# A four-layer transformer stack on one core: loops written out, weights loaded earlier, and steps moved in three stages

## The chip, the cores and the metric

The kernel runs on one core of a Trainium2 chip. The metric is the device time of one execution in microseconds (us). The engines are TensorE (PE), VectorE (DVE), ScalarE (ACT), GpSimd (POOL) and SyncE (SP, which here issues DMAs only).

## The reference, cut to what is computed

The input `x` is 8 items of 256 tokens of 256 features. Four layers each add an attention-like part and a feed-forward part and normalise after each:

```python
x = _layernorm(x + _L0_attn_ref(x, ...))   # RMS norm, Mamba-2 chunked scan (4 heads), gated
x = _layernorm(x + _L0_ffn_ref(x, ...))    # int8 weights: silu(x@Wg*s) * (x@Wu*s) @ Wd*s, 256 -> 1024 -> 256
x = _layernorm(x + _L1_attn_ref(x, ...))   # 16 heads of 128, softmax(q k^T / sqrt(128)) v @ w_o
x = _layernorm(x + _L1_ffn_ref(x, ...))    # mixture of experts
x = _layernorm(x + _L2_attn_ref(x, ...))   # Mamba scan, 512 channels x 16 states
x = _layernorm(x + _L2_ffn_ref(x, ...))    # ternary weights, silu(gate)*up, RMS norm, projection
x = _layernorm(x + _L3_attn_ref(x, ...))   # causal attention with one k and v for 16 heads, then a GELU MLP
x = _layernorm(x + _L3_ffn_ref(x, ...))    # gated, with low-rank experts
```

The mixture of experts in layer 1:

```python
_, sel = jax.lax.top_k(sigmoid(x2d @ gate_w.T), 4)            # 4 of 32 experts for each token
w = softmax(x2d @ gate_w.T)[sel]; w = w / w.sum(-1)
def _moe(x2d, Wg, Wu, Wd, cw):                                # Wg, Wu: (experts, 256, inner)
    a = silu(einsum('th,ehi->eti', x2d, Wg)) * einsum('th,ehi->eti', x2d, Wu) * cw.T[:, :, None]
    return einsum('eti,eih->th', a, Wd)
large = _moe(x, Wg, Wu, Wd, cw_large)                         # 32 experts, inner 96
small = _moe(x, cWg, cWu, cWd, cw_small)                      # 16 chunks (expert // 2), inner 128
return large + 0.05 * small
```

## The kernel before

`X` stays in SBUF. The program is a list of eight phases, `l0_attn` to `l3_ffn` (l0a, l0f, l1a, l1f, l2a, l2f, l3a, l3f in the names), and each ends at a barrier of all engines. A phase has its own buffers, and one function for each engine. The order on an engine is the order of the code, and semaphores join the engines. In all phases but l1f and l2a an engine's function is `item(0)`, `item(1)` in straight code and then `with engine.Fori(...)` over pairs of items, a loop on the engine whose body is two items (`p` picks one of two buffers).

In the feed-forward phases an item goes in steps. POOL copies its rows of `X` to `xin` (`stage`), PE transposes them into PSUM `T` (`turn`), ACT rounds them to `xh` (`keep_high`), and DVE makes the rest `xl = T - xh` (`keep_low`), so that a product of full precision is two or three products in fp32r. PE then makes gate and up for block `f` of 128 inner features (`GU`), ACT the silu `gs`, DVE `a` (the product of both) and its low part `al`, ACT its high part `ah`; `down(i - 1)` makes the output `Y` of the item before from `ah` and `al` of all its blocks, between the blocks of this item. DVE adds the residual and takes the statistics (`residual`), POOL raises the variance to -1/2 (`rstd`), and DVE writes `X` (`normalize`, L165). DVE and ACT run in steps of one block, and the numbers in `if step == 4` set where such a piece stands. In l2f POOL also sums the squares of `a` block by block (`s`), for the RMS norm.

In l0f, the int8 weights are loaded to `raw` at the phase's start and DVE casts them (L887) to `wg`, `wu`, `wd`. `raw` then serves as the ring for the weights `qkv` of l1a (`EarlyWeights`), which SP loads from there on.

In l1a an item is 16 heads, its products are L903, and the weights `wqkv` lie in two buffers `early_wqkv_h` and `early_wqkv` of 6144 columns (Q, K and V, 2048 each). The expert weights of l1f go to the same memory (`routes_over_low`, `routes_over_high`), so SP may load those for a range of columns only when the products that read these columns are over. `qk_ready` counts heads whose Q and K are made, `vc_ready` those with V. `wL[:, kc, expert, 0:192]` holds a large expert's gate (96) and up (96) side by side, `wS` the small chunks' (128 and 128), `dL` and `dS` the down weights. DVE's `routing` selects the experts of each item and numbers the tokens within each expert (`number`), and POOL scatters the rows of `X`, four copies per token, into the DRAM buffer `moe_x_rows` (`scatter`, four indirect DMAs for 128 tokens). This buffer is cleared by one DMA in l0a.

In l1f the last item's numbering and the scatters of items 6 and 7 are done first. DVE computes from the counts `n_e` a table of tiles (an expert and a place of rows for each of 95 tiles of 128 rows), SP stores it to DRAM (`moe_tiles`, L1393), reloads it as `rowi` and `rowp` (L1396), and then loads the rows of each tile (`xl`), which PE turns, multiplies with the weights of the tile's expert (L1475 large, L1478 small) and with the down weights (L1502, L1503).

In l3a step 9 of an item on ACT copies the transposed exponentials of a group of heads (`eT`, L2943) and then scales the next item's transposed input (`xT`, `keep_scaled`, L2895), which PE's projection (L2717) reads.

## Time and profile before

| what | us |
| --- | --- |
| median of three executions (lowest, highest) | 2623.26 (2620.5, 2629.05) |
| the profiled execution, its span | 2626.29, 2624.5 |
| PE busy | 2247.6, 86% of the span |
| DVE, ACT, POOL busy | 1699.0, 1443.6, 789.0 |
| bytes moved by DMA | 111.40 MB, 42 GB/s over the span |

The mean granted clock of PE is 0.932 of full speed. The phases lie, by the first instruction of each, at 0 (l0a), 258 (l0f), 400 (l1a), 939 (l1f), 1264 (l2a), 1855 (l2f), 2005 (l3a) and 2400 (l3f).

How to read it: busy times of the engines overlap, so none alone is the time. A row of the timeline gives start and duration, then engine, line, operation, `output<-inputs`, shape and a count of equal instructions run together; in brackets stands how long the engine was idle before it and what ended that. The table of waits sums these idle times by the pair of waiting line and releasing line.

### The profile page before, as it was taken

To read this page: it belongs to the slowest core of one execution; us is meant where nothing else is said; L and a number is where in the kernel's file an instruction comes from. 1 tells how busy PE (TensorE), PEld (TensorE's weight loads), DVE (VectorE), ACT (ScalarE), POOL (GpSimd) and SP (SyncE) were. 2 spreads that over 40 slices of the span, in tenths; PEclk is the share of its full clock that TensorE was granted. 3 is DMA by queue.
4 is the path that set the end of the run, shared out by engine and by line. 5 is a ranking of instruction groups with operands and counts; after the bars stand their busy time and mean duration, and the time that the engine had idled before them with its cause. 6 is when DMAs were issued, how large, how long until landed. Compare 5 with 4: busy or idle time off the path is not lost. (4 is left out here: it accounts for less than half of the span.)

```text
span 2624.5 us, 48418 instructions
## 1 busy us (share of the span) xinstructions
PE 2247.6 (86%) x15901; PEld 1944.7 (74%) x15909; DVE 1699.0 (65%) x4091; ACT 1443.6 (55%) x3765; POOL 789.0 (30%) x808
## 2 busy tenths in 40 slices
PE   6997878999999949999389889998686899987997
PEld 5875777999999939998166667767585566666886
DVE  4675776888787855552379888777465575663443
ACT  4664456777777713333377666775333565663332
POOL 1111000011111120000658777778484222221000
PEclk9888998999999969999689999999797999998999
DMA  4000111000000483332411111000300000000000
GB/s 131 1 0 13 45 54 33 1 18 18 18 18 18 103 223 114 119 103 86 130 41 49 50 47 43 33 34 1 115 0 1 1 1 0 0 0 1 1 0 32
DMA packets 98856, 111.40 MB, mean 42 GB/s; under 512 B 32330, under 2 KB 87235, under 8 KB 97621
## 3 DMA queue, kind: packets, MB, share of 16 engines
q1 hardware_dynamic: 91156, 87.23, 11.0%
q0 software_dynamic: 7488, 21.50, 2.6%
q8 instruction: 115, 1.88, 0.3%
q14 instruction: 97, 0.79, 0.1%
HBM read 79.73 MB, written 28.97 MB: 41 GB/s over the span
## 5 line engine op out<-in xcount | busy, mean ns | idle before, releaser
L1863 POOL TENSOR_TENSOR l2a_hb<-l2a_hb,l2a_Cb 128x1024 f32<-128x1024 f32 x128 | 303.1, 2379 | 112.9 <-DVE l2a_hb L2319 111.8
L2319 DVE TENSOR_TENSOR_SCAN l2a_hb<-l2a_dA,l2a_dB 128x1024 f32<-128x1024 f32 x128 | 288.3, 2274 | 62.6 <-PE l2a_dB L1944 26.8
L2173 ACT ACTIVATE l2a_dA<-l2a_delta,l2a_An 128x255 f32<-128x255 f32 x512 | 214.3, 497 | 37.3 <-DVE l2a_delta L2259 20.9
L1944 PE MATMUL l2a_dB<-l2a_diag,l2a_dxT 64*128 64x128 f32 x2048 | 188.8, 306 | 31.2 <-DVE l2a_hb L2319 18.4
L1944 PEld LDWEIGHTS l2a_dB<-l2a_diag,l2a_dxT 64*128 64x128 f32 x2048 | 139.8, 194 | 95.1 <-PE l2a_dB L1944 37.2
L903 PE MATMUL l1a_QK<-l1a_xh,early_wqkv_h 128*128 128x256 f32 x512 | 147.6, 288 | 11.1 <-issue 9.6
L903 PE MATMUL l1a_QK<-l1a_xh,early_wqkv 128*128 128x256 f32 x512 | 144.9, 283 | 0.0
L903 PE MATMUL l1a_QK<-l1a_xl,early_wqkv_h 128*128 128x256 f32 x512 | 144.8, 283 | 0.0
L1964 PE MATMUL l2a_YS<-ident,l2a_hb 128*128 128x128 f32 x1024 | 142.4, 286 | 1.0 <-POOL l2a_hb L1863 1.0
L1174 ACT ACTIVATE l1a_ex<-l1a_S,l1a_nm 128x256 f32<-128x256 f32 x256 | 119.3, 471 | 36.2 <-DVE l1a_nm L1226 36.2
L1964 PEld LDWEIGHTS l2a_YS<-ident,l2a_hb 128*128 128x128 f32 x1024 | 116.8, 146 | 12.2 <-POOL l2a_hb L1863 1.2
L2936 ACT ACTIVATE l3a_ex<-l3a_sm,l3a_nm 128x128 f32<-128x128 f32 (+1 forms) x256 | 99.0, 447 | 43.1 <-DVE l3a_nm L3073 42.4
L1209 DVE TENSOR_TENSOR l1a_qkl<-l1a_QK,l1a_qkh 128x512 fp32r<-128x512 f32 x128 | 88.3, 690 | 47.8 <-ACT l1a_qkh L1149 43.6
L1670 DVE TENSOR_TENSOR l1f_a<-l1f_s,l1f_GU 128x96 f32<-128x96 f32 x95 | 24.1, 254 | 138.8 <-ACT l1f_s L1540 138.8
L156 POOL TENSOR_TENSOR l1a_vpe<-l1a_mv,eps 128x2 f32<-128x2 f32 x8 | 1.5, 191 | 364.5 <-DVE l1a_mv L150 364.5
L903 PEld LDWEIGHTS l1a_QK<-l1a_xh,early_wqkv_h 128*128 128x128 f32 x512 | 98.1, 192 | 6.3 <-issue 6.3
L903 PEld LDWEIGHTS l1a_QK<-l1a_xl,early_wqkv_h 128*128 128x128 f32 x512 | 98.6, 193 | 5.2 <-issue 5.2
L3067 DVE TENSOR_TENSOR l3a_sm<-l3a_S,l3a_hide 128x512 f32<-128x512 f32 x96 | 65.7, 685 | 54.4 <-PE l3a_S L2786 54.3
L1478 PE MATMUL l1f_GU<-routes_over_high,l1f_xt 128*128 x380 | 98.3, 381 | 0.0
L903 PEld LDWEIGHTS l1a_QK<-l1a_xh,early_wqkv 128*128 128x128 f32 x512 | 98.2, 192 | 0.0
L1149 ACT CAST l1a_qkh<-l1a_QK 128x512 fp32r<-128x512 f32 x128 | 76.5, 598 | 35.0 <-PE l1a_QK L903 34.1
L2943 ACT COPY l3a_eT<-l3a_PT 128x512 f32<-128x512 f32 x96 | 55.4, 577 | 71.3 <-PE l3a_PT L2832 71.3
(657 smaller groups left out, 7427.3 us busy)
## 6 DMA issues: line engine op xcount, KB each, us to landing
l2a_Cb<-c_rows SPq DMA_DIRECT2D x8, 2048.0 KB, 7.0
l1f_xl<-moe_x_rows SPq DMA_DIRECT2D x95, 128.0 KB, 2.0
moe_y_rows<-l1f_yo SPq DMA_DIRECT2D x95, 128.0 KB, 1.7
l0f_raw<-in_L_attn_w_qkv_dram SPq DMA_DIRECT2D x24, 256.0 KB, 2.9
moe_x_rows<-X SPq DMA_DIRECT2D x1, 4224.0 KB, 17.3
l1f_dL<-in_L_ffn_Wd_dram SPq DMA_DIRECT2D x1, 3072.0 KB, 22.1
X<-in_L_attn_x_dram SPq DMA_DIRECT2D x8, 256.0 KB, 6.1
routes_raw<-in_L_attn_w_o_dram SPq DMA_DIRECT2D x4, 512.0 KB, 3.9
```

Of the source, the lines that this page charges most:

```text
L903: ins = pe.matmul(out, a, b, start=(first and n == 0), stop=(last and n == len(passes) - 1), **more)
L1149: nc.scalar.copy(qkh[:, h % 2].rearrange("p n t -> p (n t)"), QK[h % 2][:, :]).then_inc(qk_kept, 1)
L1174: last = nc.scalar.activation(ex[:, h % 2, j, :], S[h % 2][:, j * SEQ:(j + 1) * SEQ], ACT.Exp, bias=nm[:, h % 2, j:j + 1], scale=SCALE, ac ...
L1209: nc.vector.tensor_tensor(qkl[:, h % 2].rearrange("p n t -> p (n t)"), QK[h % 2][:, :], qkh[:, h % 2].rearrange("p n t -> p (n t)").bitcas ...
L1478: last = nc.tensor.matmul(GU[t % 2][:, 2 * EI:2 * (EI + SI)], xt[t % 2][:, kc, :], wS[:, kc, bass.ds(small, 1), :], start=(kc == 0), stop= ...
L1863: nc.gpsimd.tensor_tensor(h[:, :, :], h[:, :, :], Cb[p][:, s0:s0 + UN, :], ALU.mult).then_inc(hc_ready, 1)
L1944: last = nc.tensor.matmul(out[:, m:m + 2, j * P + a:j * P + a + HP], dxT[q][a:a + HP, j, c * P:(c + 1) * P], diag[q][a:a + HP, j, s0 + m:s ...
L1964: last = nc.tensor.matmul(YS[j][:, c * P:(c + 1) * P], hb[u % RING][:, n, j * P:(j + 1) * P], sh.ident[:, :], is_transpose=True, start=Fal ...
L2173: last = nc.scalar.activation(dA[(i * NU + u) % DAS][:, n, 1:SEQ], delta[q][:, c, 1:SEQ], ACT.Exp, scale=An[:, c, s0 + n:s0 + n + 1])
L2319: nc.vector.tensor_tensor_scan(flat(hb[u % RING]), flat(dA[(i * NU + u) % DAS]), dB[u % 2][:, :], 0.0, ALU.mult, ALU.add).then_inc(scanned, 1)
L2936: last = nc.scalar.activation(ex[:, b % NB, cols], sm[:, b % NB, cols], ACT.Exp, bias=nm[:, b % NB, n:n + 1])
L3067: nc.vector.tensor_tensor(m, S[b % 3][:, :].rearrange("p (h k) -> p h k", h=nh), hide[:, None, 2 * P - keys_n:2 * P].to_broadcast([P, nh, ...
```

## The change

1. All `Fori` loops (six phases, on PE, ACT, DVE and POOL) become Python loops, so that the engine gets straight code.
2. The loads of l0f's weights go to a new class `FirstWeights` with buffers of its own, and SP issues them in l0a. POOL casts them in l0a, one matrix each behind the `rstd` of items 2, 3 and 4. SP no longer waits for the casts before the `qkv` loads in l0f.
3. In l0f PE's `down(i - 1)` goes from behind block 2 to behind block 3, DVE's `residual` from step 4 to 5, `normalize` from 6 to 7.
4. The expert weights are turned on the host to (256, experts, inner), and in SBUF all gates lie together, then all ups. SP loads in l1a what fits in the columns of Q and K, in two batches, and the rest (Wu in the V columns, `dL`, `dS`) at the start of l1f.
5. Scatters are issued per 128 tokens. Those of the first half of item 6 go from l1f to the end of l1a, and those of the second half stand ahead of POOL's constants in l1f. POOL's last wait in l1a, for the scatters to land, is gone.
6. In l2f POOL's `stage` goes from block 2 to 0, PE's `turn` from 4 to 3, `keep_high` from step 5 to 4, `keep_low` from 6 to 5.
7. In l3a ACT scales `xT` ahead of the `eT` copy of step 9.

```diff
@@ l0_attn, SP and POOL
+            sh.first.load(sp)
             sp.wait_ge(w_loaded, 32)
...
+            def cast(src, dst):
+                if src is sh.first.raw[0]:
+                    pool.wait_ge(sh.first.loaded, 16 * 6)
+                nc.gpsimd.tensor_copy(dst[:, :, :].rearrange("p k n -> p (k n)"), src[:, :].bitcast(I8)).then_inc(sh.first.cast, 1)
...
-            with pool.Fori(1, ITEMS // 2 - 1) as it:
-                for p in range(2):
-                    item(it * 2 + p, p)
+            for i in range(2, ITEMS - 2):
+                item(i, i % 2)
+                if i < 5:
+                    cast(sh.first.raw[i - 2], (sh.first.wg, sh.first.wu, sh.first.wd)[i - 2])
@@ l0_ffn, PE and DVE
-                    if f == 2 and not first:
+                    if f == 3 and not first:
                         down(i - 1, 1 - p)
...
-            pe.wait_ge(w_cast, 3)
+            pe.wait_ge(sh.first.cast, 3)
...
-            with pe.Fori(1, ITEMS // 2) as it:
+            for it in range(1, ITEMS // 2):
                 for p in range(2):
                     item(it * 2 + p, p)
...
-                    if step == 4 and not first:
+                    if step == 5 and not first:
                         residual(i - 1)
-                    if step == 6 and not first:
+                    if step == 7 and not first:
                         normalize(ph, dve, i - 1)
...
-            for src, dst in zip(raw, (wg, wu, wd)):
-                nc.vector.tensor_copy(dst[:, :, :].rearrange("p k n -> p (k n)"), src[:, :].bitcast(I8)).then_inc(w_cast, 1)
@@ l1_attn, SP
-            sp.wait_ge(qk_ready, (ITEMS - 1) * NH + half_freed)
-            experts(routes.wL, "", 0, freed(half_freed))
...
-            sp.wait_ge(vc_ready, ITEMS * NH)
-            experts(routes.wL, "", freed(2 * NH), routes.wL.shape[2])
-            for kc in range(KC):
-                sp.dma_start(routes.dS[:, :, kc, :], w["L1_ffn_cWd"].rearrange("e i (k c) -> k i e c", k=KC)[kc]
-                             ).then_inc(routes.small_down_loaded, 16)
+            part, some = NH * DH, NH // 2 * DH
+            sp.wait_ge(qk_ready, (ITEMS - 1) * NH + NH // 2)
+            routes.load(sp, ((0, some), (part, part + some)))
             sp.wait_ge(qk_ready, ITEMS * NH)
+            routes.load(sp, ((0, 2 * part),))
@@ l1_attn, POOL
+            pool.wait_ge(routing.idx_ready, ITEMS - 1)
+            scatter(nc, pool, sh, ITEMS - 2, 0)
             rstd(ph, pool, ITEMS - 1)
-            pool.wait_ge(routes.rows_out, 16 * (ITEMS - 2) * NT * routes.TOPK)
@@ l1_ffn, SP, POOL and PE
-            sp.dma_start(dL[:, :, :], w["L1_ffn_Wd"].rearrange("e i n -> i e n")).then_inc(down_loaded, 16)
+            routes.load(sp, ((0, sh.early.columns),))
+            sp.dma_start(dL[:, :, :], w["L1_ffn_Wd"]).then_inc(down_loaded, 16)
+            for kc in range(KC):
+                sp.dma_start(dS[:, :, kc, :], w["L1_ffn_cWd"].rearrange("i e (k c) -> k i e c", k=KC)[kc]).then_inc(routes.small_down_loaded, 16)
             sp.wait_ge(tab_ready, 1)
...
-            scatter(nc, pool, sh, None, 0, ITEMS - 2)
+            scatter(nc, pool, sh, ITEMS - 2, 1)
...
-                    nc.tensor.matmul(GU[t % 2][:, 0:2 * EI], xt[t % 2][:, kc, :], wL[:, kc, bass.ds(large, 1), :],
+                    nc.tensor.matmul(GU[t % 2][:, 0:2 * EI], xt[t % 2][:, kc, :], wL[:, kc, :, bass.ds(large, 1), :],
@@ l2_ffn, POOL, PE, ACT and DVE
-                    if f == 2:
+                    if f == 0:
                         stage(ph, pool, i + 1)
...
-                    if f == 4:
+                    if f == 3:
                         turn(ph, pe, i + 1)
...
-                    if step == 5:
+                    if step == 4:
                         keep_high(ph, act, i + 1, xh[1 - p])
...
-                if step == 6:
+                if step == 5:
                     keep_low(ph, dve, i + 1, xh[1 - p], xl[1 - p], xl_ready)
@@ l3_attn, ACT
+                    if step == 9:
+                        keep_scaled(act, i + 1, 1 - p)
                     if step >= 1:
                         b = step - 1
                         act.wait_ge(e_turned, done(b))
...
-                    if step == 9:
-                        keep_scaled(act, i + 1, 1 - p)
@@ class Routes
+    def load(self, sp, free):
+        for dst, name in ((self.wL, ""), (self.wS, "c")):
+            _, _, _, count, wide = dst.shape
+            for n, side in ((0, "Wg"), (1, "Wu")):
+                for begin, end in free:
+                    at = n * count * wide
+                    experts = [e for e in range(count) if begin <= at + e * wide and at + (e + 1) * wide <= end
+                               and (name, n, e) not in self.asked]
+                    if experts:
+                        first, last = experts[0], experts[-1] + 1
...
+                        for kc in range(KC):
+                            sp.dma_start(dst[:, kc, n, first:last, :], self.w["L1_ffn_" + name + side][kc * P:(kc + 1) * P, first:last, :]
+                                         ).then_inc(self.gate_up_loaded, 16)
```

**The order on SP at the end of l1a and the start of l1f.** Before (`Wg` and `Wu` are the large experts' weights, `cWd` the small down weights; the branch L1389 is the start of l1f):

```order
L999 DMA routes_over_high<-in_L_ffn_cWg_dram 128x4x128 x2
L999 DMA routes_over_high<-in_L_ffn_cWu_dram 128x4x128 x2
L999 DMA routes_over_high<-in_L_ffn_cWg_dram 128x4x128 x2
L999 DMA routes_over_high<-in_L_ffn_cWu_dram 128x4x128 x2
L999 DMA routes_over_low<-in_L_ffn_Wg_dram 128x11x96 x2
L999 DMA routes_over_low<-in_L_ffn_Wu_dram 128x11x96 x2
L1017 DMA routes_over_high<-in_L_ffn_cWd_dram 128x16x128 x2
L916 UNCONDITIONAL_BRANCH
L1389 UNCONDITIONAL_BRANCH
L1391 DMA l1f_dL<-in_L_ffn_Wd_dram 96x32x256
L1393 DMA moe_tiles<-l1f_tabi 128x4
L1396 DMA l1f_rowi<-moe_tiles 1x512
```

After (the branch L1360 is the start of l1f):

```order
L3556 DMA routes_over_low<-in_L_ffn_Wg_dram 128x1152 x2
L3556 DMA routes_over_low<-in_L_ffn_Wu_dram 128x960 x2
L3556 DMA routes_over_high<-in_L_ffn_cWg_dram 128x1024 x2
L3556 DMA routes_over_high<-in_L_ffn_cWu_dram 128x1024 x2
L908 UNCONDITIONAL_BRANCH
L1360 UNCONDITIONAL_BRANCH
L3556 DMA routes_over_low<-in_L_ffn_Wu_dram 128x2112 x2
L1363 DMA l1f_dL<-in_L_ffn_Wd_dram 96x8192
L1365 DMA routes_over_high<-in_L_ffn_cWd_dram 128x16x128 x2
L1367 DMA moe_tiles<-l1f_tabi 128x4
```

The last weights of gate and up and the small down weights moved behind the start of l1f, and each stands in longer rows.

**The order on DVE in item 1 of l0f,** from the split of the next item's input (`xl`) on. Before:

```order
L128 TENSOR_TENSOR l0f_xl<-l0f_T,l0f_xh 128x512
L864 SCALAR_TENSOR_TENSOR l0f_a<-l0f_GU,l0f_su,l0f_gs 128x256
L870 TENSOR_TENSOR l0f_al<-l0f_a,l0f_ah 128x256
L853 TENSOR_TENSOR l0f_ys<-l0f_Y,l0f_sd 128x256 x2
L135 TENSOR_TENSOR l0f_r<-X,l0f_ys 128x512
L146 BN_STATS l0f_stats<-l0f_r 128x6 x2
L148 MEMSET l0f_carrier 128x1
L150 BN_AGGR l0f_mv<-l0f_stats 128x2 x2
L864 SCALAR_TENSOR_TENSOR l0f_a<-l0f_GU,l0f_su,l0f_gs 128x256
L870 TENSOR_TENSOR l0f_al<-l0f_a,l0f_ah 128x256
L864 SCALAR_TENSOR_TENSOR l0f_a<-l0f_GU,l0f_su,l0f_gs 128x256
L870 TENSOR_TENSOR l0f_al<-l0f_a,l0f_ah 128x256
```

After:

```order
L128 TENSOR_TENSOR l0f_xl<-l0f_T,l0f_xh 128x512
L858 SCALAR_TENSOR_TENSOR l0f_a<-l0f_GU,first_su,l0f_gs 128x256
L864 TENSOR_TENSOR l0f_al<-l0f_a,l0f_ah 128x256
L858 SCALAR_TENSOR_TENSOR l0f_a<-l0f_GU,first_su,l0f_gs 128x256
L864 TENSOR_TENSOR l0f_al<-l0f_a,l0f_ah 128x256
L847 TENSOR_TENSOR l0f_ys<-l0f_Y,first_sd 128x256 x2
L135 TENSOR_TENSOR l0f_r<-X,l0f_ys 128x512
L146 BN_STATS l0f_stats<-l0f_r 128x6 x2
L148 MEMSET l0f_carrier 128x1
L150 BN_AGGR l0f_mv<-l0f_stats 128x2 x2
L858 SCALAR_TENSOR_TENSOR l0f_a<-l0f_GU,first_su,l0f_gs 128x256
L864 TENSOR_TENSOR l0f_al<-l0f_a,l0f_ah 128x256
```

The five rows of the residual and its statistics moved behind one more pair of `a` and `al`.

**The order on ACT in item 1 of l3a,** around step 9. Before:

```order
L2936 ACTIVATE l3a_ex<-l3a_sm,l3a_nm 128x256 x2
L2943 COPY l3a_eT<-l3a_PT 128x512
L2936 ACTIVATE l3a_ex<-l3a_sm,l3a_nm 128x256 x2
L2943 COPY l3a_eT<-l3a_PT 128x512
L2936 ACTIVATE l3a_ex<-l3a_sm,l3a_nm 128x256 x2
L2943 COPY l3a_eT<-l3a_PT 128x512
L2895 ACTIVATE l3a_xT<-l3a_T,late_b,late_g 128x256 x2
L2936 ACTIVATE l3a_ex<-l3a_sm,l3a_nm 128x256 x2
L2943 COPY l3a_eT<-l3a_PT 128x512
```

After:

```order
L2912 ACTIVATE l3a_ex<-l3a_sm,l3a_nm 128x256 x2
L2921 COPY l3a_eT<-l3a_PT 128x512
L2912 ACTIVATE l3a_ex<-l3a_sm,l3a_nm 128x256 x2
L2921 COPY l3a_eT<-l3a_PT 128x512
L2912 ACTIVATE l3a_ex<-l3a_sm,l3a_nm 128x256 x2
L2871 ACTIVATE l3a_xT<-l3a_T,late_b,late_g 128x256 x2
L2921 COPY l3a_eT<-l3a_PT 128x512
L2912 ACTIVATE l3a_ex<-l3a_sm,l3a_nm 128x256 x2
L2921 COPY l3a_eT<-l3a_PT 128x512
```

The two activations that make `xT` moved ahead of one copy `eT`.

## Rows read from the trace of the kernel before

**Rows 1.** Windows: l1a and l3a; busy us (instructions) of each engine, clock, DMA, GB/s.

```profile
400.00:939.00 539.00, 508.77 (x4258) 505.73 (x4258) 428.51 (x1255) 395.77 (x1173) 67.18 (x90) 0.97 0.14 38
...
2005.00:2400.00 395.00, 346.98 (x2152) 252.77 (x2152) 227.32 (x550) 218.50 (x488) 89.21 (x117) 0.97 0.00 0
```

**Rows 2.** Waits of PE in l0f: us in total, times, longest.

```profile
PE l0f_Y L786 <- DVE l0f_al L870: 14.8, 7, 6.5
PE l0f_GU L799 <- DVE l0f_wd L887: 8.5, 1, 8.5
```

**Rows 3.** Waits of PE, and timelines of PE and DVE, in l1a.

```profile
PE l1a_QK L903 <- issue: 9.6, 2, 4.8
...
656.18 0.37 PE L903 MATMUL l1a_QK<-l1a_xh,early_wqkv_h 128*128 128x256 f32 x1 [4.83 <-issue]
...
625.82 0.73 DVE L165 TENSOR_SCALAR X<-l1a_r,l1a_mv,l1a_rstd 128x256 f32 x2
...
694.08 0.72 DVE L165 TENSOR_SCALAR X<-l1a_r,l1a_mv,l1a_rstd 128x256 f32 x2
...
756.55 0.73 DVE L165 TENSOR_SCALAR X<-l1a_r,l1a_mv,l1a_rstd 128x256 f32 x2
```

**Rows 4.** Waits of PE, and timeline of POOL, in l2f.

```profile
PE l2f_GU L2478 <- DVE l2f_xl L128: 10.5, 6, 1.8
...
1945.60 0.61 POOL L2413 TENSOR_TENSOR l2f_s<-l2f_a 128x256 f32<-128x256 f32 x1 [1.18 <-DVE l2f_a L2557]
```

**Rows 5.** Waits of PE, and timeline of ACT, in l3a.

```profile
PE l3a_T L2717 <- ACT l3a_xT L2895: 14.1, 9, 1.6
...
2214.20 0.59 ACT L2943 COPY l3a_eT<-l3a_PT 128x512 f32<-128x512 f32 x1
```

**Rows 6.** Timeline of DVE at the start of l0f.

```profile
260.52 0.69 DVE L128 TENSOR_TENSOR l0f_xl<-l0f_T,l0f_xh 128x512 fp32r<-128x512 f32 x1 [3.48 <-ACT l0f_xh L121]
264.83 1.23 DVE L887 CAST l0f_wg<-l0f_raw 128x2048 fp32r<-128x2048 int8 x1 [3.62 <-DMA l0f_sd<-in_L_ffn_s_down_dram]
```

**Rows 7.** Timelines of POOL and DVE in l0a.

```profile
44.02 2.49 POOL L292 TENSOR_TENSOR l0a_Dx<-l0a_xtm,l0a_Db 128x512 f32<-128x512 f32 x2 [23.82 <-issue]
...
124.41 2.49 POOL L292 TENSOR_TENSOR l0a_Dx<-l0a_xtm,l0a_Db 128x512 f32<-128x512 f32 x2 [1.24 <-ACT l0a_xtm L491]
...
55.82 1.29 DVE L671 TENSOR_TENSOR l0a_yu<-l0a_W,l0a_Dx 128x512 f32<-128x512 f32 x2
```

**Rows 8.** Timelines of DVE and PE in an item of l0f.

```profile
332.33 0.48 DVE L864 SCALAR_TENSOR_TENSOR l0f_a<-l0f_GU,l0f_su,l0f_gs 128x256 f32<-128x256 f32 x1 [2.78 <-ACT l0f_gs L826]
...
333.66 0.48 DVE L864 SCALAR_TENSOR_TENSOR l0f_a<-l0f_GU,l0f_su,l0f_gs 128x256 f32<-128x256 f32 x1
...
342.14 0.39 PE L786 MATMUL l0f_Y<-l0f_wd,l0f_ah 128*128 128x256 f32 x1 [1.59 <-DVE l0f_al L870]
```

**Rows 9.** Timelines of DVE and SP's queue, end of l1a, start of l1f.

```profile
930.87 0.73 DVE L165 TENSOR_SCALAR X<-l1a_r,l1a_mv,l1a_rstd 128x256 f32<-128x256 f32 x2 [1.11 <-POOL l1a_rstd L158]
...
950.52 0.19 DVE L1565 COPY l1f_n_e<-l1f_YP 128x32 f32<-128x32 f32 x1 [3.86 <-POOL l1f_tau L1420]
...
934.05 4.28 SPq L1017 DMA_DIRECT2D routes_over_high<-in_L_ffn_cWd_dram  x2
939.45 2.31 SPq L1391 DMA_DIRECT2D l1f_dL<-in_L_ffn_Wd_dram  x1
955.26 0.35 SPq L1393 DMA_DIRECT2D moe_tiles<-l1f_tabi  x1
962.24 0.31 SPq L1396 DMA_DIRECT2D l1f_rowi<-moe_tiles  x1
```

**Rows 10.** DMA from 939 to 965 us, in 40 slices, and its sum.

```profile
GB/s 328 294 290 291 290 291 289 342 314 263 232 211 247 258 361 314 307 350 375 340 306 244 353 252 358 257 227 355 323 356 294 327 348 174 208 25 0 6 0 0
DMA packets 6969, 6.76 MB, mean 260 GB/s; under 512 B 450, under 2 KB 6454, under 8 KB 6968
```

**Rows 11.** Costliest groups: the small gate and up products of l1f.

```profile
L1478 PE MATMUL l1f_GU<-routes_over_high,l1f_xt 128*128 x380 | 98.3, 381 | 0.0
```

More of the change, by code:

```diff
@@ L432, in _ @@
             item(1, 1)
-            with pe.Fori(1, ITEMS // 2 - 1) as it:
+            for it in range(1, ITEMS // 2 - 1):
                 for p in range(2):
@@ L704, in _ @@
             item(1, 1)
[L705 removed]
+            for it in range(1, ITEMS // 2 - 1):
                 for p in range(2):
@@ L840, in _ @@
             keep_high(ph, act, 0, xh[0])
-            act.wait_ge(w_loaded, 16 * 6)
+            act.wait_ge(sh.first.loaded, 16 * 6)
             item(0, 0, first=True)
             item(1, 1)
-            with act.Fori(1, ITEMS // 2) as it:
+            for it in range(1, ITEMS // 2):
                 for p in range(2):
@@ L970, in of @@
                 item(1, 1, range(NH), second=True)
-                with engine.Fori(1, ITEMS // 2) as it:
-                    for p in range(2):
-                        item(it * 2 + p, p, range(NH))
+                for i in range(2, ITEMS):
+                    item(i, i % 2, range(NH))
                 end()
@@ L2429, in _ @@
             item(1, 1)
-            with pool.Fori(1, ITEMS // 2) as it:
+            for it in range(1, ITEMS // 2):
                 for p in range(2):
@@ L2490, in _ @@
             item(1, 1)
-            with pe.Fori(1, ITEMS // 2) as it:
+            for it in range(1, ITEMS // 2):
                 for p in range(2):
@@ L2523, in _ @@
             item(1, 1)
-            with act.Fori(1, ITEMS // 2) as it:
+            for it in range(1, ITEMS // 2):
                 for p in range(2):
@@ L2574, in _ @@
             item(1, 1)
-            with dve.Fori(1, ITEMS // 2) as it:
+            for it in range(1, ITEMS // 2):
                 for p in range(2):
@@ L2958, in _ @@
             item(1, 1)
-            with act.Fori(1, ITEMS // 2) as it:
+            for it in range(1, ITEMS // 2):
                 for p in range(2):
@@ L3156, in _ @@
             item(1)
-            with pool.Fori(1, ITEMS // 2) as it:
+            for it in range(1, ITEMS // 2):
                 for p in range(2):
@@ L3243, in _ @@
             item(1, 1)
-            with pe.Fori(1, ITEMS // 2) as it:
+            for it in range(1, ITEMS // 2):
                 for p in range(2):
@@ L3305, in _ @@
             item(1, 1)
-            with act.Fori(1, ITEMS // 2) as it:
+            for it in range(1, ITEMS // 2):
                 for p in range(2):
@@ L3401, in _ @@
             item(1, 1)
-            with dve.Fori(1, ITEMS // 2) as it:
+            for it in range(1, ITEMS // 2):
                 for p in range(2):
```

127 lines of the change are left out of this document (65 added, 62 removed).

## The prediction

> **What bounds the kernel now.** I first read the busy time by stage [rows 1]. A stage is one phase, between two barriers, and TensorE (PE) is the fullest engine in each (94% of the attention of layer 1, l1a; 88% of that of layer 3, l3a). So what can be gained is an end of a wait of PE, and I read, stage by stage, what PE waits for, and then in the timeline what that work itself waited for. What the reader is to see: in l0f PE waits 14.8 us for `al` and once 8.5 us for the cast of `wd` [rows 2]; in l1a 9.6 us for "issue", which is nothing that the profile shows [rows 3]; in l2f for `xl`, the split of the next item's input [rows 4]; in l3a 14.1 us for ACT's `xT` [rows 5]. And between l1a and the first tile of l1f PE has nothing to do.
>
> **The change part by part.** A positive number is time saved on the path.
>
> *1. Start of l0f: 7.1.* DVE makes `xl` by 260.52 + 0.69 = 261.2, waits for the loads, and casts three matrices from 264.83 on, 1.2 us each [rows 6]; PE starts behind the third, 8.5 us later than it could for the rest [rows 2]: at 268.4. With the weights loaded and cast in l0a, PE can start behind `xl`, at 261.3: 7.1. The casts go to POOL in l0a, one each behind the rstd of items 2, 3 and 4. No row has this cast on POOL. From below: DVE's 1.23 us [rows 6]. From above: POOL's product of two inputs takes 2.49/2 = 1.25 us for 128x512 [rows 7], so 5.0 for 128x2048. I take 3. POOL's next work, `Dx`, now begins 1.24 us after the work before it, so it comes 2 to 4 us late. But DVE reads it late: the first `Dx` is done at 46.5, and the addition that reads it starts at 55.8 [rows 7], so some 9 us are hidden: cost 0. The six loads (0.9 MB) stand ahead of the clearing of the MoE rows, which is waited for only in item 2 of l1a: cost 0.
>
> *2. Re-timed down in l0f: 7.6.* The ring of an item: DVE's `a` of step 3 at 332.33, `a` of step 4 at 333.66, and so on to the last `al`, then PE's down at 342.14 after a wait of 1.59 [rows 8]; its 32 matmuls, the gate and up of the fourth block, silu, and again step 3. With down behind f == 3 the ring closes at the `a` of 333.66 instead: 1.33 shorter, less some 0.13 for DVE's residual, which moves a step too. 1.2 x 6 items, and 0.4 between items 1 and 2: 7.6. The waits can pay it: 14.8 in seven times is 2.1 an item [rows 2]. Bounds: 0 (another part of the ring takes over) and 1.6 x 7 = 11.
>
> *3. Straight code: 13.0 in l1a, 0.7 elsewhere.* DVE's normalise marks the items: 694.08 to 756.55 is 62.47, but 625.82 to 694.08 is 68.26. In the long one PE stands still for 4.83 us at 656.18, for "issue" [rows 3], at the first product of an item, where the loop branches back. It does so twice, 9.6 us [rows 3], for a loop over items 2 to 7 that branches back twice. 68.26 - 62.47 = 5.8; the second costs about the same or, with what it lets idle, some 7. I take 13.0 for the two, with 11.6 and 13.5 as bounds. Items 0 and 1, straight code already, have no such row. Only l1a has it: its loop body holds 2 x 4258/8 = 1064 matmuls and as many weight loads, that of l3a 2 x 2152/8 = 538 [rows 1], and the others less. Their edges I put at 0.7 together. The Trainium skill ("Runtime: NRT & Kernel Launch", Instruction fetch mechanics) says that PE holds 2048 instructions, fetches ahead in order only, and stalls when a taken branch leaves that window. By that rule, too, the stall goes with this branch.
>
> *4. Expert weights and scatters around the end of l1a: 1.5.* In l1a SP still issues the small down weights at 934.05, for 4.28 us, and l1f starts at 939.45, although DVE has normalised the last item by 930.87 + 0.73 = 931.6 [rows 9]. In the new order SP's last load of l1a is due with the last `QK`, so l1f starts some 1.1 us after DVE, at 932.7: 6.7 earlier. Of the scatters, four leave the head of l1f; the copy of `n_e` waited 3.86 us for the constants behind them [rows 9], so the table of tiles is ready another 3.8 earlier, and stored at about 955.26 - 10.5 = 944.8. But PE waits for what comes back from that store, and before it landed only at 962.2, 7.0 us after its issue [rows 9]. The queue that it stands in now gets, at 932.7, V-column weights (2.2 MB), `dL` (3.1 MB) and `dS` (2.1 MB), with 12 scatters (1.6 MB) beside it: 9.0 MB. At the mean of 260 GB/s of this stretch that is 34.6 us, ending at 967; its best slice shows 375 [rows 10], which gives 24 us, 957. The runs of 8 and 32 KB are nearer to the upper, `dS` (512 B) and the scatters to the lower: I take 28, 960.7, so that 1.5 of the 10.5 is left. Bounds: -4.5, and 10.5 if the store does not stand behind the loads. The Trainium skill ("DMA: Bandwidth & Descriptors", the table at its head) puts full rate at 512 B a piece and more. By that rule the old pieces of 384 B were dear and the new ones cheap; the sum stays, since those in l1a are over before anyone waits for them.
>
> PE's operand of gate and up is now two pieces of 96 columns with a gap. The down product already reads `dS` with a gap and `dL` without: cost 0. As a bound: a tenth more on 2 x 380 matmuls of 98.3/380 = 0.26 us [rows 11] is 20.
>
> *5. l2f: 5.3.* PE waits 10.5/6 = 1.75 us an item for `xl` [rows 4]. POOL's copy at f == 0, PE's turn at f == 3 and both splits a step earlier take that off. But POOL is nearly full: in a period of 15.25 it waits once, 1.18 us, for the `a` that DVE makes after normalising [rows 4]. Its copy of the next input, 0.8, now falls into that wait, and the rest of its round stays: 0.75 x 7 = 5.3. Bounds: 0 and 10.5.
>
> *6. l3a: 4.6.* PE's projection waits 14.1/9 = 1.57 us for `xT`, which ACT starts behind the `eT` copy of 0.59 [rows 5]. The swap saves that copy: 0.58 x 8 = 4.6. That `eT` comes 1.0 late, and PE reads it some 4 us after. Bounds: 0 and 4.7.
>
> **Sum.** 7.1 + 7.6 + 13.7 + 1.5 + 5.3 + 4.6 = 39.8. The profiled execution took 2626.3 us (its span 2624.5), 3.0 over the median of 2623.3: from the median, 2583.5.
>
> **The rivals.**
> *A. The store of tiles is not held by the loads.* For it: separate transfers need not end in order. Against it: 7.0 us for 2 KB behind `dL`. 9 more: 2575.
> *B. The stalls go with the length of the code, not with the branch.* For it: nothing in the profile releases "issue". Against it: items 0 and 1. 13.7 less: 2597.
> *C. The re-timings give nothing,* since a neighbouring wait takes over, as POOL partly does in l2f. Against it: each ring was followed row by row. 17.5 less: 2601.
> *D. Slower: POOL's cast is slow.* It stands ahead of `Dx` three times. Beyond some 9 us each, every microsecond is paid three times; from 9 + 39.8/3 = 22 us a cast, 11 ns a column against 2.4 in the product's row [rows 7], the kernel is slower. The Trainium skill ("GPSIMD Engine Reference") counts about 12 cycles an element for loops that branch on data; a cast that ran so would come near this.
> *E. A tenth more for each gate and up product* (above): 20 back, 2603.
>
> **How the numbers follow.** A measurement of this kernel tells about 0.3%, 8 us, from no change. Forecast 0.62 (its own range 2577 to 2591), A 0.12 (2575), B 0.07 (2597), C 0.09 (2601, or part of it), E 0.04 (2603), D 0.03 (over 2631), two or three of B, C and E together 0.03 (about 2618, the same). The range that leaves out no more than 2 in 10 reaches from 2570 (A with more of the bound of l2f) to 2600. Faster 0.94, same 0.03, slower 0.03.
>
> **What would show it.** Right: the first gate product of l0f 2.6 us after its first turn, no cast row on DVE, and PE's waits for `al` down from 14.8 to some 7; in l1a normalise rows 62.3 to 62.5 apart throughout and no "issue" row of 4 us; in l1f a store of tiles that takes over 10 us to land; in l2f periods near 14.5 with POOL's wait gone; in l3a `xT` right behind the exp. Wrong: a cast on POOL of over 9 us, gaps in l1a that stay, a store that lands in 2 us, tiles further apart than before.

## The result and the profile after

| | before | changed |
| --- | --- | --- |
| median of four executions, us | 2626.16 | 2601.30 |
| lowest, highest | 2620.50, 2630.61 | 2596.28, 2603.39 |
| span of the profiled execution | 2624.5 | 2599.6 |

The medians lie 24.9 us apart, where 39.8 were forecast. The ratio of the times is 0.9902, with a 95% interval of 0.9885 to 0.9919. The time, 2601.3, lies just above the forecast range (2570 to 2600).

DVE's last normalise of each stage (the last L165 row of its timeline) cuts the two profiles alike. The table gives the stretch from the one mark to the next.

| stretch | before | changed | saved | forecast |
| --- | --- | --- | --- | --- |
| l0a | 256.3 | 263.9 | -7.5 | 0 |
| l0f | 141.5 | 135.9 | 5.6 | 14.7 |
| l1a | 533.1 | 519.8 | 13.3 | 13.0 |
| end of l1a to the first tile's turn | 36.4 | 44.3 | -8.0 | 1.5 |
| tiles, and l2a up to the first turn of l2f | 887.9 | 882.8 | 5.1 | 0 |
| l2f from there | 145.8 | 138.5 | 7.3 | 5.3 |
| l3a | 396.8 | 390.7 | 6.1 | 4.6 |
| l3f | 217.0 | 214.1 | 2.9 | 0.7, with all other edges |
| sum | | | 24.8 | 39.8 |

So the totals of three stretches came out as forecast or better (l1a, l2f, l3a; in l2f partly by luck, as run 8 shows), and three terms failed: l0a, which was to cost nothing, the re-timing in l0f, and the start of l1f.

The windows of l1a and l3a (busy us and instructions of PE, its weight loads, DVE, ACT and POOL, clock, DMA share, GB/s) stand against [rows 1]; PE does the same work in less span.

```profile
401.40:924.70 523.30, 503.89 (x4258) 500.12 (x4258) 426.26 (x1255) 395.06 (x1173) 71.39 (x95) 0.99 0.10 35
1987.00:2377.50 390.50, 347.76 (x2152) 253.95 (x2152) 224.91 (x555) 217.09 (x488) 90.64 (x122) 0.96 0.00 1
```

**l0a.** Timelines of POOL and DVE in the changed kernel. The cast that the prediction put at 3 us takes 1.89, and `Dx` follows right behind it. But the two instructions of DVE's normalise, 0.73 us together in the items without a cast but one, take 3.22 here.

```profile
123.69 1.89 POOL L301 CAST first_wg<-first_raw 128x2048 fp32r<-128x2048 int8 x1
123.78 3.22 DVE L165 TENSOR_SCALAR X<-l0a_r,l0a_mv,l0a_rstd 128x256 f32<-128x256 f32 x2 [1.08 <-POOL l0a_rstd L158]
```

Taken one by one, each of the two instructions ends about 0.15 us behind an instruction of POOL that was already running or had begun just before it: the first behind the cast, the second behind the first product of `Dx`, which now has no gap ahead of it.

```profile
123.78 1.95 DVE L165 TENSOR_SCALAR X<-l0a_r,l0a_mv,l0a_rstd 128x256 f32<-128x256 f32 x1 [1.08 <-POOL l0a_rstd L158]
125.54 1.31 POOL L293 TENSOR_TENSOR l0a_Dx<-l0a_xtm,l0a_Db 128x512 f32<-128x512 f32 x1
125.65 1.35 DVE L165 TENSOR_SCALAR X<-l0a_r,l0a_mv,l0a_rstd 128x256 f32<-128x256 f32 x1
```

The kernel before shows the same once, in item 6, where the two products of `Dx` come right behind `rstd`, without any cast. The sign could have been read there:

```profile
232.40 2.53 POOL L292 TENSOR_TENSOR l0a_Dx<-l0a_xtm,l0a_Db 128x512 f32<-128x512 f32 x2
232.47 2.60 DVE L165 TENSOR_SCALAR X<-l0a_r,l0a_mv,l0a_rstd 128x256 f32<-128x256 f32 x2 [1.08 <-POOL l0a_rstd L158]
```

**l0f.** The waits of PE, against [rows 2]. The wait for the casts is gone and of those for `al` only the last is left, as the prediction's signs asked. But PE now waits 21.6 us for POOL's copy of the input, where 6.9 was before.

```profile
PE l0f_T L106 <- POOL l0f_xin L96: 21.6, 7, 5.6
PE l0f_Y L780 <- DVE l0f_al L864: 6.4, 1, 6.4
PE l0f_GU L793 <- DVE l0f_xl L128: 1.5, 1, 1.5
```

Around one of these waits, timelines of DVE, POOL and PE. To be read downwards: DVE's statistics of the finished item, POOL's two instructions for `rstd`, POOL's copy of the next input behind them, PE's turn behind the copy.

```profile
337.97 0.75 DVE L146 BATCH_NORM_STATS2 l0f_stats<-l0f_r 128x6 f32<-128x256 f32 x2
339.09 0.55 POOL L156 TENSOR_TENSOR l0f_vpe<-l0f_mv,eps 128x2 f32<-128x2 f32 x1 [12.46 <-DVE l0f_mv L150]
339.71 0.69 POOL L158 TENSOR_TENSOR l0f_rstd<-l0f_vpe,minus_half 128x2 f32<-128x2 f32 x1
340.35 1.03 POOL L96 COPY l0f_xin<-X 128x512 f32<-128x512 f32 x1
341.44 0.33 PE L106 MATMUL l0f_T<-ident,l0f_xin 128*128 128x128 f32 x1 [2.75 <-POOL l0f_xin L96]
```

And two items side by side in windows: with the same work one takes 14.8, the other 16.3 us. The granted clock is 1.00 of 2.4 GHz in the first and on average 0.90 in the second, which has a stretch at the lower level, 1.2 GHz, some 1 to 4 us behind the end of the wait of 2.75 us at its head. An item of the kernel before took 15.3 us at 1.00. So with the wait, but at the full clock, the new order is 0.5 us an item shorter; the clock takes 1.5 back in every second one. Why it falls in only every second one isn't shown.

```profile
326.80:341.60 14.80, 12.05 (x101) 11.84 (x102) 12.32 (x33) 8.39 (x22) 2.21 (x3) 1.00 0.23 72
341.60:357.90 16.30, 13.55 (x102) 13.35 (x102) 12.30 (x33) 8.37 (x22) 2.21 (x3) 0.90 0.22 65
```

**l1a.** Two normalise rows of DVE, against [rows 3]: 62.23 apart, and no pair of full items more than 62.26. No wait for "issue" is left among PE's waits there.

```profile
628.46 0.73 DVE L165 TENSOR_SCALAR X<-l1a_r,l1a_mv,l1a_rstd 128x256 f32<-128x256 f32 x2
690.69 0.73 DVE L165 TENSOR_SCALAR X<-l1a_r,l1a_mv,l1a_rstd 128x256 f32<-128x256 f32 x2
```

**Start of l1f.** SP's queue and PE's first turn of a tile in the changed kernel, against [rows 9]. DVE's last normalise of l1a starts at 919.47. l1f starts 5.3 later (8.6 before), and DVE has the table of tiles ready at 936.5. The second load of small down weights starts at 926.77 and holds SP until 947.72, so the store is issued only then. It lands by 957.35, when the reload behind it is issued: 37.9 us behind l1a's last normalise, where the kernel before took 31.4 and the prediction's sum has 29.8.

```profile
924.73 0.81 SPq L3556 DMA_DIRECT2D routes_over_low<-in_L_ffn_Wu_dram  x2
925.58 0.42 SPq L1363 DMA_DIRECT2D l1f_dL<-in_L_ffn_Wd_dram  x1
926.05 21.67 SPq L1365 DMA_DIRECT2D routes_over_high<-in_L_ffn_cWd_dram  x2
947.76 5.81 SPq L1367 DMA_DIRECT2D moe_tiles<-l1f_tabi  x1
957.35 0.30 SPq L1370 DMA_DIRECT2D l1f_rowi<-moe_tiles  x1
957.70 0.23 SPq L1370 DMA_DIRECT2D l1f_rowp<-moe_tiles  x1
961.63 0.39 SPq L1378 DMA_DIRECT2D l1f_xl<-moe_x_rows  x1
...
963.79 0.45 PE L1434 MATMUL l1f_T<-ident,l1f_xl 128*128 128x128 f32 x1 [32.66 <-DMA l1f_xl<-moe_x_rows]
```

The instructions that end l1a (name, count, duration in ns three times, start twice), by the line of the phase. POOL's drain takes 5.1 us; DVE's, behind its last normalise, 0.8.

```profile
L908 POOLq DRAIN  x1: 5092/5092/5092, 918.7 to 918.7; - x1
L908 DVEq DRAIN  x1: 769/769/769, 919.5 to 919.5; - x1
```

**l2f and l3a.** Waits of PE, against [rows 4] and [rows 5]. In l2f the wait for `xl` is gone, and what is left is behind POOL's sum of squares; the items lie 14.43 to 14.45 apart but for the first pair, 15.68 (15.2 to 15.9 before). In l3a they lie 44.22 apart (45.1).

```profile
PE l2f_SS L2431 <- POOL l2f_s L2394: 14.2, 8, 4.6
PE l2f_T L106 <- POOL l2f_xin L96: 10.6, 1, 10.6
...
PE l3a_T L2693 <- ACT l3a_xT L2871: 8.2, 9, 1.3
```

### The profile page after: what moved, and what is told of

Its sections match the earlier page's. It is cut to its first block and busy times, and to the rows that moved or that the text cites. A ratio compares the mean times of both kernels' runs of the same rounds, so it can differ in the third digit from the quotient of the medians.

```text
span 2599.6 us, 46478 instructions
## 1 busy us (share of the span) xinstructions
PE 2244.9 (86%) x15901; PEld 1943.4 (75%) x15909; DVE 1696.3 (65%) x4088; ACT 1440.3 (55%) x3765; POOL 799.2 (31%) x811
## 5 line engine op out<-in xcount | busy, mean ns | idle before, releaser
L1920 PE MATMUL l2a_dB<-l2a_diag,l2a_dxT 64*128 64x128 f32 x2048 | 188.1, 305 | 31.4 <-DVE l2a_hb L2295 18.6
L1940 PE MATMUL l2a_YS<-ident,l2a_hb 128*128 128x128 f32 x1024 | 141.0, 284 | 1.0 <-POOL l2a_hb L1839 1.0
L1140 ACT ACTIVATE l1a_pr<-l1a_ex,l1a_rz 128x256 f32<-128x256 f32 x128 | 65.3, 510 | 50.3 <-DVE l1a_rz L1191 47.5
## 6 DMA issues: line engine op xcount, KB each, us to landing
l1f_dL<-in_L_ffn_Wd_dram SPq DMA_DIRECT2D x1, 3072.0 KB, 22.4
```

The lines of the kernel that those rows point to most:

```text
L1140: nc.scalar.activation(pr0[:, h % 2, :], ex[:, h % 2, 0, :], ACT.Copy, scale=rz[:, h % 2, 0:1]).then_inc(probs_ready, 1)
L1920: last = nc.tensor.matmul(out[:, m:m + 2, j * P + a:j * P + a + HP], dxT[q][a:a + HP, j, c * P:(c + 1) * P], diag[q][a:a + HP, j, s0 + m:s ...
L1940: last = nc.tensor.matmul(YS[j][:, c * P:(c + 1) * P], hb[u % RING][:, n, j * P:(j + 1) * P], sh.ident[:, :], is_transpose=True, start=Fal ...
```

## The experiments

Each run gave one time, beside one of the kernel before on the same chip, and a profile, except where more is said. Runs 3, 6, 7 and 8 are of one chip, on which the kernel before took 2655.0 us and these took 2624.9, 2635.3, 2617.8 and 2629.1. There the items of l1a with scatters in them, from the third on, lay 65 to 67 us apart instead of 62.2: PE stood idle for about 2 us in each, and in many of them its granted clock was 0.97 or 0.98. No trace of the kernel before was kept on that chip, so the reason stays open, and these runs are read by their other stretches.

**1. Casts behind `Dx`.** In POOL's `item` of l0a:

```diff
                 for j in range(NT): ... Dx ...
+                if 2 <= i < 5:
+                    cast(sh.first.raw[i - 2], ...)
                 if left > 1:
                     inverse_rms(pool, i + 2)
                 rstd(ph, pool, i)
```

> The changed kernel, with POOL's three int8 casts of l0a behind the Dx products of items 2, 3 and 4 instead of behind their rstd. In the changed kernel each cast (1.89 us) runs while DVE normalises, and that DVE row takes 3.22 instead of 0.73 us. Theory (the two engines disturb each other on SBUF while DVE runs this kind of work): the casts still take 1.9, but DVE then works from PSUM; the normalise rows take 0.73 again, the items of l0a lie 27.3 apart instead of 29.6, and l0a's last normalise comes at about 257 instead of 263.9. Rival (the loads of the weights, issued early, or a POOL that is late, slow l0a): the items stay near 29.6 apart. Second rival (every DVE instruction is disturbed): another DVE row grows by about 2, and the end stays near 262 to 264.

l0a's last normalise comes at 257.5 instead of 263.9, its items 27.3 apart; 2598.5 us in all. POOL's cast and DVE around it:

```profile
128.02 1.89 POOL L303 CAST first_wu<-first_raw 128x2048 fp32r<-128x2048 int8 x1
124.38 0.74 DVE L165 TENSOR_SCALAR X<-l0a_r,l0a_mv,l0a_rstd 128x256 f32<-128x256 f32 x2 [1.08 <-POOL l0a_rstd L158]
128.32 1.61 DVE L591 SCALAR_TENSOR_TENSOR l0a_ax<-l0a_dtr 128x8 f32<-128x8 f32 x1
```

The normalise takes 0.74 again. The cast still blocks DVE: the small instruction at 128.32, 0.17 us without it (in the kernel before), takes 1.61 and ends with the cast. Its neighbour at 128.12, `dtr`, which reads PSUM, takes 0.17 beside the same cast. There DVE had waited for PE anyway, so the path hardly sees it. `Dx`, which the cast held up for about half a microsecond in the changed kernel, stands ahead of it here, so the normalise meets neither.

**2. POOL's input copy one item earlier in l0f.**

```diff
             def item(i, p, first=False):
-                stage(ph, pool, i + 1)
+                if i + 2 <= ITEMS:
+                    stage(ph, pool, i + 2)
                 if not first:
                     rstd(ph, pool, i - 1)
             stage(ph, pool, 0)
+            stage(ph, pool, 1)
```

> The changed kernel, with POOL's copy of the input in l0f made one item earlier in POOL's order: item i copies i + 2, ahead of the rstd of i - 1, where the changed kernel copies i + 1 behind the rstd of i - 2. Theory (with the residual a step later, rstd is later, the copy behind it too, and PE's turn waits 2.75 us an item for it): that wait is gone, PE's clock no longer drops in every second item, and the period, now 15.65 on average, becomes 13 to 14 (DVE's 12.2 of work plus little). l0f is shorter by 10 to 16 us. Rival (the ring of a, al and down is at fault as before): the wait moves to al, the period stays at 15.2 or above.

l0f takes 128.2 instead of 135.9; the items lie 14.3 apart, a little above the 13 to 14 expected. PE's waits:

```profile
PE l0f_Y L782 <- DVE l0f_al L866: 10.4, 7, 6.4
PE l0f_T L106 <- POOL l0f_xin L96: 5.3, 1, 5.3
PE l0f_GU L795 <- DVE l0f_a L860: 4.5, 5, 0.9
```

The copy is no longer waited for but once, at the start; `al` is again, 0.7 us an item, and the granted clock is 1.00 in every item. The 7.7 us less are fewer than the 10 to 16 expected, though the theory's sign, the wait for the copy gone, came true.

**3. `down` behind block 2 again,** with the residual in step 4 and the normalise in step 6:

```diff
-                    if f == 3 and not first:
+                    if f == 2 and not first:
                         down(i - 1, 1 - p)
...
-                    if step == 5 and not first:
+                    if step == 4 and not first:
                         residual(i - 1)
-                    if step == 7 and not first:
+                    if step == 6 and not first:
```

> The changed kernel with down, residual and normalise of l0f where the kernel before has them (down behind block 2, residual in step 4, normalise in step 6); everything else stays changed, the input copy of POOL too. Theory (the step later residual delays rstd and the copy behind it): PE's wait for the copy falls back to 0.2 us, the clock holds, and the period is 15.2 to 15.4 again, against 15.65 in the changed kernel: l0f is 1 to 3 us shorter than the changed kernel's 135.9. Rival (the re-timing helped, and something else of the change slows l0f): the period grows above 15.65.

l0f takes 134.5, its items 15.25: the weights loaded and cast ahead give 141.5 - 134.5 = 7.0 us (7.1 forecast), of which straight code may be 0.5 (run 8), and the re-timing as it stands costs 1.4. With POOL's earlier copy the two together are worth 134.5 - 128.2 = 6.3. That is not the re-timing alone, since the earlier copy was not run without it; but PE waits for the copy only 1.6 us in the items of this run, so little of the 6.3 can be the copy's own.

**4. V-column and small down weights in l1a.** SP waits for the last V and issues both loads there; the large down weights alone stand at the start of l1f.

```diff
             routes.load(sp, ((0, 2 * part),))
+            sp.wait_ge(vc_ready, ITEMS * NH)
+            routes.load(sp, ((0, sh.early.columns),))
+            for kc in range(KC): ... dma_start(routes.dS[:, :, kc, :], ...)
```

> The changed kernel, with the weights for the V columns and the small down weights loaded at the end of l1a again (behind the last V), in the new long runs; the large down weights stay at the start of l1f. Theory (SP itself is stuck for 21 us in issuing the second small down load, so the table of tiles, ready at 936.4, is stored at 947.8, and the scatters starve beside it): SP is free when the table is ready; the store is issued at the table's readiness, lands in 2 to 4 us, and the first tile's turn comes 28 to 32 us behind DVE's last normalise of l1a instead of 44.3: 12 to 16 us less in all. l1f's start does not come later, since POOL's drain (5.1 us) holds it anyway. Rival (the bytes bound the stretch, whoever issues them): the same 9 MB are under way, only 8 us earlier; the turn comes 36 to 38 us behind.

The turn comes 34.1 us behind the last normalise: 10.2 less, between the two. SP issues the store at once (at 933.93, the table being ready at 933.90), but it takes 9.3 us to land, behind the large down weights:

```profile
922.11 0.35 SPq L1366 DMA_DIRECT2D l1f_dL<-in_L_ffn_Wd_dram  x1
933.93 0.35 SPq L1368 DMA_DIRECT2D moe_tiles<-l1f_tabi  x1
943.25 0.29 SPq L1371 DMA_DIRECT2D l1f_rowi<-moe_tiles  x1
```

The row of GB/s in 40 slices of 930 to 949 us of this run shows that traffic:

```profile
GB/s 802 138 0 9 431 664 138 0 69 414 483 138 0 9 267 828 138 0 9 52 242 382 381 380 293 173 319 345 268 69 13 0 0 4 0 0 0 0 112 164
```

Up to the twentieth slice, while the large down weights (rows of 32 KB) are moved, slices of 400 to 828 stand beside slices of 0 to 138. It comes in lumps, or the profile books a long packet's bytes at one moment; the row doesn't tell which. 2589.8 us in all.

**5. Table stored and reloaded from ACT's queue.** The wait for `tab_ready`, the store, the wait for it and the two reloads move from SP behind ACT's `Exp`, word for word.

> The changed kernel, with the store of the table of tiles and its two reloads issued by ACT instead of SP; all weights stay at the start of l1f. If SP's issue alone held the store (theory), it lands within 3 us of the table's readiness, about 17 us behind l1a's last normalise; the first tile still waits for its rows, which SP loads behind the weights, and for the scatters, so that the turn comes about 38 to 42 us behind instead of 44.3. If the queue is one for all engines, or the bytes hold it (rival), the store lands after the weights, near 957, and nothing changes.

The turn stays at 44.6 behind. The store, now issued 1.4 us behind the table, takes 14.8 us to land:

```profile
936.68 0.35 ACTq L1500 DMA_DIRECT2D moe_tiles<-l1f_tabi  x1
951.47 0.48 ACTq L1503 DMA_DIRECT2D l1f_rowi<-moe_tiles  x1
```

So SP's block was real, but not alone. Another engine's queue needs 14.8 us for its 2 KB, so that they land only 4.7 us sooner behind l1a's last normalise. SP's first load of rows then waits for scatters until 957.3; they took up to 18 us to land here and in the changed kernel. And PE's first turn comes 5.6 us behind that load, where it was 2.2 in the changed kernel; why isn't shown. 2600.4 us in all.

**6 and 7. The large down weights behind the table, or in pieces.** Both start from run 4. In one the load of `dL` stands behind the reload of the table; in the other it becomes

```diff
-            sp.dma_start(dL[:, :, :], w["L1_ffn_Wd"]).then_inc(down_loaded, 16)
+            for e in range(0, E, 2):
+                sp.dma_start(dL[:, e:e + 2, :], w["L1_ffn_Wd"][:, e:e + 2, :]).then_inc(down_loaded, 16)
```

> The changed kernel with V-column and small down weights loaded in l1a (as in the run before this one, where the table's store still took 9.3 us to land, behind the large down weights), and now the large down weights issued behind the reload of the table. Theory (the long transfer of 3.1 MB holds the store and the scatters): the store lands in 2 to 3 us, the reload too, the first tile's turn comes 28 to 31 us behind l1a's last normalise instead of 34.1; the first down product may then wait for its weights, 18 to 22 us from their issue, which gives back 3 to 8 us. Rival (the scatters alone hold the tiles): the turn stays at 33 to 34.

> As the run with V-column and small down weights in l1a, but with the large down weights in 16 transfers of two experts (rows of 2 KB) instead of one of 32 KB rows; same bytes, same place. Theory (long rows are moved in large packets, and small transfers wait behind them: slices of 828 GB/s stand beside slices of 0): the store and the scatters land sooner, the turn comes 30 to 32 us behind instead of 34.1. Rival (bytes are bytes): it stays at 34, or SP's issue of 16 transfers makes it later.

Behind the table, the store lands in 1.4 us and the reload in 3.2, but the rows' first load is issued only at 984.4, 18 us behind that of `dL`, when the scatters have landed; the turn comes 45.7 behind, 11.6 later than in run 4. The last scatter was issued at 967.6, just behind `dL`, and SP waited for it until 984.4, 16.8 us; in run 4 the last was issued at 939.7 and had landed by 947.3. So the store is free as expected, but the 28 to 31 us are missed: the long load did not hold the store alone, it held the scatters.

```profile
961.85 0.34 SPq L1367 DMA_DIRECT2D moe_tiles<-l1f_tabi  x1
963.27 0.32 SPq L1370 DMA_DIRECT2D l1f_rowi<-moe_tiles  x1
966.43 0.33 SPq L1372 DMA_DIRECT2D l1f_dL<-in_L_ffn_Wd_dram  x1
984.40 1.52 SPq L1379 DMA_DIRECT2D l1f_xl<-moe_x_rows  x2
```

In pieces, with the same bytes at the same place, the store lands in 6.3 us and the turn comes 31.0 behind:

```profile
948.15 7.58 SPq L1367 DMA_DIRECT2D l1f_dL<-in_L_ffn_Wd_dram  x16
959.98 0.35 SPq L1369 DMA_DIRECT2D moe_tiles<-l1f_tabi  x1
966.27 0.28 SPq L1372 DMA_DIRECT2D l1f_rowi<-moe_tiles  x1
969.69 2.64 SPq L1380 DMA_DIRECT2D l1f_xl<-moe_x_rows  x3
```

**8. Straight code alone,** in the kernel before: every `with engine.Fori(...) as it` becomes `for it in range(...)`.

> The kernel before with straight code in place of all loops, and nothing else. Theory: l1a's items lie 62.2 to 62.5 apart, 13 us less; l3a's items 44.8 to 45.0 instead of 45.1 and l3f's 23.92 instead of 24.07, so that straight code in all gives 14 to 16 us and the swap on ACT in l3a the other 0.6 of its 0.87 us an item. Rival (the whole 0.87 an item in l3a is the swap's): l3a stays at 45.1.

In l1a the two gaps of 4.8 us are gone: PE's longest wait for "issue" is 1.0. Nothing else was changed, so they went with the loops. The 13 us themselves can't be read on this chip (above); they are read from the changed kernel, 62.2 an item. Elsewhere straight code gives more than the 0.7 forecast: l0a 254.7 (256.3 before), l0f 141.0 (141.5), l2f from its first turn 142.1 (145.8), with items of 15.06 (15.2 to 15.9), l3a 396.3 (396.8), with items of 44.99 (45.1), l3f 214.6 (217.0). That is 8.7 us together, of which l2f's 3.7 is the least sure: its stretch differs by up to 4.6 us between runs with the same code there. In all the run took 25.9 us less than the kernel before on its chip, where 14 to 16 were expected. One execution stands against one, and where the rest came from is open.

**9. ACT's swap in l3a undone.**

```diff
-                    if step == 9:
-                        keep_scaled(act, i + 1, 1 - p)
                     if step >= 1: ... eT copy ...
+                    if step == 9:
+                        keep_scaled(act, i + 1, 1 - p)
```

> The changed kernel with ACT's scaling of xT in l3a behind the eT copy of step 9 again. Items of l3a lie 45.09 apart before, 44.99 with straight code alone, 44.22 in the changed kernel. Theory (the swap gives 0.77 an item): 44.95 to 45.05. Rival (something else of the change gives more than the copy's 0.58): 44.8 or less.

44.99, as with straight code alone. The swap is worth 0.77 an item, more than the copy's 0.59. 2609.4 us in all.

**10. All scatters of l1a in l1f.**

```diff
-                    for j in range(NT):
-                        scatter(nc, pool, sh, i - 2, j)
-            scatter(nc, pool, sh, ITEMS - 2, 0)
...
+            for i in range(ITEMS - 1): ... scatter(nc, pool, sh, i, j)
```

> The changed kernel with every scatter of l1a issued at the start of l1f instead, so that POOL issues no indirect DMA in l1a. It is slower as a whole, since l1f's first tile waits for some 52 more scatters, about 66 us; what is asked is only how soon l1f starts. Theory (POOL's drain at the end of a phase takes 5.1 us where the phase had indirect DMAs and 0.8 where it had none): the drain takes 0.8, and l1f's first instruction comes 1.0 to 1.2 us behind DVE's last normalise (0.74 long), as in the other phases, instead of 4.5. Rival (the drain follows from what else POOL does in l1a, or the barrier waits for something else): it stays at 4.5 us.

Without indirect DMAs in l1a POOL's drain takes 0.8 us, and l1f starts 1.0 behind the end of the normalise. The drain in l1a of the other runs took 5.1 us, and 6.6 to 7.1 in runs 4, 6 and 7.

```profile
L908 POOLq DRAIN  x1: 792/792/792, 913.9 to 913.9; - x1
```

The first scatter of l1f, 0.7 us behind the start in the changed kernel, then comes 3.7 behind it (at 920.08, start 916.42): some of the cost moves there. The kernel takes 2661.5 us, with the scatters in a row (2655.3 for the kernel before on that chip). The items of l1a, now without scatters, lay 62.2 apart.

**11. The four pieces together** (runs 1, 2, 4 and 7) in five executions, and the changed kernel again on the same chip in four.

> The changed kernel with four pieces moved, none taken out: POOL's casts in l0a behind the Dx products; POOL's input copy in l0f one item earlier; the V-column and small down weights back in l1a; the large down weights in 16 transfers of two experts. From the single runs: 6.3 us in l0a, 7.7 in l0f, 13.4 at the start of l1f (turn 31 us behind l1a's last normalise instead of 44.3). Theory (the four are independent): 27 us less than the changed kernel, 2572 to 2576 where the kernel before takes 2626, a ratio to it of 0.980. Rival (what one gains another waits for, as the granted clock of PE in l1a, which then starts earlier behind busier work): half of it, 0.985.

> The changed kernel unchanged, on the same chip as the mended one. All theories: ratio to the kernel before 0.9885 to 0.9919, as measured.

Four mended: 2574.1 us, ratio 0.9801, interval 0.9783 to 0.9818. The changed kernel: 2599.5 us, ratio 0.9890, interval 0.9866 to 0.9913. The kernel before on that chip: 2627.5. The stretches are close to those of the single runs: l0a 255.2, l0f 128.4, the first tile's turn 30.9 behind l1a. The pieces add up: 25.4 us of the 27 expected, and the median lies within the 2572 to 2576 forecast.

## Why the prediction was off

*Start of l0f, 7.1: right* (7.0 in run 3). **Its price, "cost 0", failed.** I asked how late POOL's next work would be, and it was hidden as I said. What I didn't ask is what the cast does to an engine that neither waits for POOL nor is waited for: it blocks DVE while it runs. The items with a cast are 2.4 us longer, and l0a in all 7.5; run 1 gets back 6.3. The rival on this side, a cast so slow that `Dx` comes late, had the right instruction and the wrong way. The Trainium skill has it ("SBUF — State Buffer", SBUF: two separate sides): GpSimd and VectorE share one pair of SBUF ports as an exclusive lock, held for the whole instruction, and on VectorE's side only an instruction in a two-port mode or with two inputs in SBUF needs it. The rows agree: the normalise and the 8-column instruction of run 1, which work in SBUF alone, are held, and `dtr`, with an input in PSUM, is not. They show the price too. It is not the cast's 1.89 us but 2.49, because the lock is met twice: once at the cast, and once at the `Dx` product that the cast had moved up against the normalise.

*Re-timed down, 7.6: the ring was right, the step "saves 1.2 an item" failed.* It named DVE's residual as what moves with it, and not who reads the residual: POOL's rstd, and in POOL's order the copy of the next input behind it, and PE's turn. That is one engine further than I went. The wait of 2.75 us an item ate 0.7 of the 1.2, and in every second item the granted clock was 0.90 behind it, which took another 1.5 us: more than was left. With the copy out of the way, and its own small share in it, the step gives 0.9 an item (15.25 in run 3, 14.3 in run 2).

*Straight code in l1a, 13.0: right,* 13.3, with the two long items 6.0 and 7.1 us shorter. *Elsewhere 0.7: too small,* 8.7 in one execution (run 8); I looked at how the items alternate and not at what every item of a loop pays.

*Start of l1f, 1.5: two steps failed, and one rival with them.* "l1f starts some 1.1 us after DVE": it starts 4.5 after, since POOL's drain takes 5.1 us where indirect DMAs went ahead (run 10). The same drain (4.6) was in the profile of before, hidden under SP. And the store was to land at 960.7, bound by the bytes. But the store, for which the table was ready at 936.5, was issued only at 947.8, because SP was held 21 us in issuing the second small down load; and the scatters, which I had counted as bytes only, took up to 18 us to land beside the long rows. The rates that I used came from rows of 1 KB. In rows of 32 KB the same 3.1 MB landed hardly sooner (22.4 us in the changed kernel and 18.6 in run 4, 22.1 before) and let the small transfers wait. The Trainium skill ("DMA: Bandwidth & Descriptors", Queues, rings and completion order) says that each DMA engine takes its queues in turn and changes between them only at the end of a packet. By that rule a small transfer from another engine's queue has to wait for the long packets' ends. Run 5 agrees as far as it goes (14.8 us for 2 KB), and run 7 shows what shorter rows give (31.0 instead of 34.1). That it is the packet, and not another effect of the length of a row or of the bytes beside it, is argued, not shown. Rival A (9 us better) would have needed the store to pass; it did not, even from another engine.

*l2f, 5.3: right as a total (7.3), partly by luck.* The items lie at 14.44 where 14.5 was forecast, but straight code alone brings them from 15.2 and more to 15.06 and the stretch down by 3.7; the re-timing itself gives 0.62 an item where 0.75 was forecast, and the stretch another 3.6. *l3a, 4.6: too small:* the swap is worth 0.77 an item and straight code 0.1. Of the other rivals, B fell (no gap is left in l1a), D fell (the cast takes 0.92 ns a column), E fell (the tiles lie as close as before, 2.8 us), and C came true in l0f alone, by the copy and the clock and not by a part of the ring.

What stays open: from the first tile's turn to l2f's first turn the changed kernel took 882.8 us and the kernel before 887.9, but the other runs with the changed code there took 884.4 to 891.3. So it isn't shown that these 5 us, for which no step of the change was priced, are the change's. The stretches without them sum to 19.7, while the medians of several executions lie 24.9 and, in run 11, 27.9 apart. Nor is it settled why SP was held for 21 us.
